# Two attention blocks in one program on one core: new set-up, a split value product, new orders at the layer change and at the end

## The reference, cut to what matters

```python
def _L0_cond_ref(x, emb, src_mask, ...):                  # H = 16 heads of 32
    xn = layer_norm(x, norm_w, norm_b)
    q = xn @ q_w + q_b ; k = xn @ k_w + k_b
    att = softmax(einsum('bnhl,bmhl->bnmh', q, k) + (1.0 - mask) * -1000000.0, axis=2)
    v = (xn @ v_w + v_b) * mask
    y = einsum('bnmh,bmhl->bnhl', att, v)
    scale, shift = split(silu(emb) @ emb_w + emb_b)
    h = layer_norm(y, sb_norm_w, sb_norm_b) * (1.0 + scale) + shift
    return x + silu(h) @ out_w + out_b

def _L1_cond_ref(x, emb, src_mask, ...):                  # H = 8 heads of 64
    q = softmax(xn @ Wq + bq, over a head's 64 features)
    k = softmax(xn @ Wk + bk + (1 - mask) * -1e6, over the tokens)
    att = einsum('bnhd,bnhl->bhdl', k, v)                 # 64 x 64 per head
    y = einsum('bnhd,bhdl->bnhl', q, att)                 # then the same tail
```

## Time and profile before

| | |
|---|---|
| time before | 1080.86 us, median of 3 runs (1080.82 to 1081.48) |
| the profiled execution | 1084.61 us, of which the span of the trace is 1082.8 us |
| TensorE busy (products) | 1030.0 us, 95% of the span, 8554 instructions |
| DVE, ACT, POOL busy | 770.1, 609.6 and 588.7 us |
| mean granted TensorE clock | 0.991 of full speed |

### The profile page before, as it was taken

The page is one execution under the profiler, slowest core; times in us unless marked ns, Lnnn a source line. Parts: engine busy times, 40 slices in busy tenths (PEclk is TensorE's granted clock), DMA queues, the critical chain, the costliest instruction groups (busy, mean ns, idle before and its releaser), DMA issues. The chain is left out here.

```text
span 1082.8 us, 26060 instructions
## 1 busy us (share of the span) xinstructions
PE 1030.0 (95%) x8554; PEld 897.0 (83%) x8554; DVE 770.1 (71%) x1349; ACT 609.6 (56%) x2018; POOL 588.7 (54%) x870
## 2 busy tenths in 40 slices
PE   2999999999999999999997899999999999999996
PEld 2678889888888888988886778888888888888885
DVE  3567666766667666676678687777887787778775
ACT  2375678766776668766694544444444444444443
POOL 3453465445654465544653576556655565666623
PEclk9999999999999999999999899999999999999999
DMA  7833102211012110111113312222111121112111
GB/s 210 283 138 120 62 26 63 63 41 61 24 63 63 41 55 30 63 54 50 43 45 112 103 44 65 64 65 63 54 39 62 53 63 53 53 63 63 44 40 39
DMA packets 46401, 74.24 MB, mean 69 GB/s; under 512 B 8304, under 2 KB 14576, under 8 KB 46352
## 3 DMA queue, kind: packets, MB, share of 16 engines
q1 hardware_dynamic: 46352, 73.63, 21.4%
HBM read 56.80 MB, written 16.81 MB: 68 GB/s over the span
## 5 line engine op out<-in xcount | busy, mean ns | idle before, releaser
L468 POOL TENSOR_SCALAR stat<-stat 128x1 f32<-128x1 f32 x128 | 34.9, 273 | 351.5 <-DVE stat L898 330.4
L1294 PE MATMUL bank<-xt_hi,w_hi 128*128 128x256 f32 x768 | 220.4, 287 | 1.5 <-DVE xt_lo L921 1.5
L1296 PE MATMUL bank<-xt_hi,w_lo 128*128 128x256 f32 x768 | 215.5, 281 | 0.0
L1295 PE MATMUL bank<-xt_lo,w_hi 128*128 128x256 f32 x768 | 215.4, 281 | 0.0
L634 ACT ACTIVATE prob<-prob,neg_max 128x128 f32<-128x128 f32 x512 | 198.5, 395 | 10.5 <-DVE neg_max L935 10.5
L1294 PE MATMUL bank<-w_hi,xt_hi 128*128 128x512 f32 x384 | 157.2, 409 | 3.6 <-DVE w_lo L859 2.0
L1296 PE MATMUL bank<-w_hi,xt_lo 128*128 128x512 f32 x384 | 151.9, 396 | 0.0
L1295 PE MATMUL bank<-w_lo,xt_hi 128*128 128x512 f32 x384 | 151.3, 394 | 0.0
L1294 PEld LDWEIGHTS bank<-xt_hi,w_hi 128*128 128x128 f32 x768 | 146.5, 191 | 5.0 <-issue 1.9
L1295 PEld LDWEIGHTS bank<-xt_lo,w_hi 128*128 128x128 f32 x768 | 146.1, 190 | 1.3
L1296 PEld LDWEIGHTS bank<-xt_hi,w_lo 128*128 128x128 f32 x768 | 145.9, 190 | 0.0
(11 more groups left out here) (113 smaller groups left out, 2341.8 us busy)
## 6 DMA issues: line engine op xcount, KB each, us to landing
x_in<-in_x_dram SPq DMA_DIRECT2D x32, 256.0 KB, 2.8
x_res<-in_x_dram SPq DMA_DIRECT2D x32, 256.0 KB, 2.9
between_layers<-x_res SPq DMA_DIRECT2D x32, 256.0 KB, 2.0
x_in<-between_layers SPq DMA_DIRECT2D x32, 256.0 KB, 3.2
x_res<-between_layers SPq DMA_DIRECT2D x30, 256.0 KB, 2.6
out_dram<-x_res SPq DMA_DIRECT2D x30, 256.0 KB, 2.0
room<-in_L_cond_W_emb_dram SPq DMA_DIRECT2D x8, 512.0 KB, 6.9
prob<-in_L_cond_emb_w_dram SPq DMA_DIRECT2D x4, 512.0 KB, 7.6
```

The source lines that it names most:

```text
L468: pool.tensor_scalar(v[:, 8:9], v[:, 7:8], EPS, None, ALU.add).then_inc(s[a_in].sem, 1)
L1294: pe.matmul(o, a_hi, b_hi, start=start, stop=False)
L1295: pe.matmul(o, a_hi, b_lo, start=False, stop=False)
L1296: return pe.matmul(o, a_lo, b_hi, start=False, stop=stop)
```

## The change

What it does, by part:

1. **Set-up.** The two norm rows are loaded by ACT's queue as one row of 2 KB each (`norm_row`) and TensorE spreads them: a product of a row of ones with the row (`ones_row`), into banks 2 and 3, from which ACT copies them to `wide` (`norm_rows_out`). SP loads both x tiles and then the weights; three other spread rows and some columns go later in its list. A first small ACT instruction (`warm`) draws the table load forward. `first_norm` does both sequences on DVE in two instructions each. The low parts of chunks 0 and 1 of the query weight move to POOL. TensorE's first queries (`first_queries`) do the four high x high products of a block first and wait for the low parts only then. Keys come ahead of the mask's transposes.
2. **Value product.** In `step0` (all 15 passes) and `step_mixed` the last of its four chunks (three matmuls of 512 columns) stands behind the last `turn_probs` of the pair, where it stood ahead of it.
3. **Change of layers.** In step 14 SP loads the x tiles of pair 17 right away, where they stood behind five other loads in step 15; the low parts of the second block's value weight move from DVE to POOL, those of its query weight are cut in two halves on ACT and DVE; in `step_mixed` DVE does both `k_soft` ahead of the second sequence's `softmax`.
4. **The end.** `drain` puts the outputs of the last two pairs later on TensorE and DVE, in other banks; the x tiles for pair 30's residual are loaded into `xn`, which is free by then, so they need not wait for a store.

The diff, cut:

```diff
@@ banks @@
-        LATE = dict(O=(5, 3))
-        LATER = dict(O=(6, 3))
-        DRAIN = SECOND | dict(V=(0, 6), Q=(2, 2), KT=(4, 5), QT=(1, 0), KV=(4, 5), Y=(2, 1), H=(0, 4), O=(5, 7))
+        LATE = dict(O=(1, 2))
+        LATER = SECOND | dict(H=(5, 7), O=(5, 6))
+        DRAIN = SECOND | dict(V=(0, 3), Q=(2, 4), KT=(6, 7), QT=(2, 4), KV=(0, 3), Y=(6, 0), H=(3, 4), O=(7, 0))
@@ SP: start @@
-                load_x(0, pair(0), 0)
-                load_norm(0)
+                load_front(0, pair(0))
                 load_weight(0, WQ)
-                load_x(0, pair(0), 1)
                 load_weight(0, WK)
-                load_wide(0, WV, VALUE_BIAS[0], par_in[0])
...
@@ SP: step0 @@
+                if i == G - 2:
+                    load_front(1, pair(G + 1))
+                    sp.wait_ge(mask_saved, 32)
+                    load_mask_pair(n)
+                    sp.wait_ge(w_split[1][WK], 1)
+                    load_weight(1, WQ)
...
                 store(0, k, 0)
@@ SP: drain @@
+                    sp.wait_ge(*done(s["xn_turned"], f + b))
+                    sp.wait_ge(*done(s["res_full"], k + (b - GROUP)))
+                    sp.dma_start(xn[:, b, :], sequence(middle, k + (b - B))).then_inc(s["res_in"][b].sem, 16)
@@ POOL @@
+            def low_part(l, j, some, last):
+                for c in some:
+                    pool.wait_ge(w_high[l][j], c + 1)
+                    low = pool.tensor_tensor(lo[l][j][:, c], raw[l][j][c // 2][:, c % 2], hi[l][j][:, c].bitcast(F32),
+                                             ALU.subtract)
+                if last:
+                    low.then_inc(w_split[l][j], 1)
@@ POOL: start @@
+                for b in range(GROUP):
+                    rsqrt(b, 0, "aggr", "rstd_a", "rstd_b", "neg_mean", pair(0) + b, "xn_turned")
+                low_part(0, WQ, (0, 1), True)
@@ POOL: step0 @@
                 v_mask(f, slot, 1)
+                if i == G - 2:
+                    low_part(1, WV, (0, 1), False)
...
                 add_shift(k, 1)
+                if i == G - 2:
+                    low_part(1, WV, (2, 3), True)
@@ ACT @@
+            for i, v in enumerate((layers[0]["nw"], layers[0]["nb"])):
+                act.dma_start(norm_row[:, i, :], v.rearrange("(o n) -> o n", o=1)).then_inc(row_in, 16)
+            act.wait_ge(once, 2)
+            act.activation(mask_now[:], minus_half[:], ACT.Identity).then_inc(warm, 1)
...
+                norm_rows_out()
+                high_part(0, WQ, (0, 1, 2))
                 xt_high(f, 0, 0)
+                high_part(0, WQ, (3,))
                 xt_high(f, 0, 1)
@@ DVE: first_norm(b) @@
+                dve.wait_ge(row_out, 1)
+                dve.scalar_tensor_tensor(out=row, in0=x_in[:, b, :], scalar=v[:, 10:11], in1=w, op0=ALU.add, op1=ALU.mult
+                dve.wait_ge(row_out, 2)
+                dve.scalar_tensor_tensor(out=row, in0=row, scalar=v[:, 9:10], in1=bias, op0=ALU.mult, op1=ALU.add
@@ DVE: step0, i == G - 2 @@
                     low_part(1, WK, (2, 3))
-                    low_part(1, WV)
@@ DVE: step_mixed @@
                 k_soft(f, slot, 0)
+                k_soft(f, slot, 1)
+                softmax(k, 1, (0, 1))
                 stats1(n, 0)
-                softmax(k, 1, (0, 1, 2))
+                softmax(k, 1, (2,))
                 output(FIRST, late + (-1), 1)
                 softmax(k, 1, (3,))
-                k_soft(f, slot, 1)
                 stats1(n, 1)
                 sums_inverse(k, 0)
+                low_part(1, WQ, (0, 1))
                 y_norm(0, k, 1 - slot, 0)
...
+                low_part(1, WQ, (2, 3))
                 film_scale(k, 0)
-                low_part(1, WQ)
@@ PE: start @@
+                for i in range(2):
+                    claim(2 + i, times(row_out, i + 1))
+                    pe.matmul(bank[2 + i][:], ones_row[:], norm_row[:, i, :], start=True, stop=True).then_inc(row_pe, 1)
                 for b in range(GROUP):
                     turn(f, b)
-                need(0, WQ)
-                queries0(f, 0, 0)
-                queries0(f, 0, 1)
+                first_queries(f)
@@ PE: step0 (step_mixed alike) @@
-                values(0, FIRST, f, slot, 0)
+                values(0, FIRST, f, slot, 0, range(C - 1))
                 turn_probs(k, 1, (2, 3))
+                values(0, FIRST, f, slot, 0, (C - 1,))
                 turn_yn(0, k, 0)
                 weigh(k, 1 - slot, 1)
@@ PE: drain @@
                 turn_k(k, 0, 1)
-                output(1, LATE, k + (-GROUP), 0)
                 keys(1, f, 1, 0)
...
                 keys_values(f, 1, 1, DRAIN)
+                turn_yn(1, k, 0, LATER)
+                turn_q(f, 1, 0, DRAIN)
+                output(1, LATE, k + (-GROUP), 0)
+                turn_q(f, 1, 1, DRAIN)
                 query(f, 0, DRAIN)
-                turn_q(f, 1, 1, DRAIN)
+                turn_yn(1, k, 1, LATER)
                 query(f, 1, DRAIN)
+                output(1, LATE, k + (-GROUP), 1)
+                turn_yn(1, f, 0, DRAIN)
                 output(1, LATER, k, 0)
-                turn_yn(1, f, 0, DRAIN)
+                turn_yn(1, f, 1, DRAIN)
                 output(1, LATER, k, 1)
```

209 lines of the change are left out of this document (118 added, 91 removed).

## The result

The changed kernel takes 1072.66 us, median of 4 runs (1071.39 to 1074.12); the kernel before took 1081.17 beside it (1080.82 to 1083.82). The ratio is 0.9924, with a 95% interval of 0.9911 to 0.9938: 8.2 us faster, where the forecast was 14.2 us and 1066.7. The time lies inside the range of 8 in 10 (1056 to 1074), 6 us above the forecast, but outside the band of 1062 to 1071 to which the forecast gave 60%; it lies in the band of "given back".

A forecast was written before the change was run, and what follows sets the result against it. The prediction took TensorE's work, 1030.0 us of a 1082.8 us span, as the bound. Its terms, -9.8 + 2.9 - 5.0 - 2.3 = -14.2 us, taken off 1080.86 gave 1066.7 us, with an 8-in-10 range of 1056 to 1074.

The forecast's parts named there:

- given back: Rival, 18%: waits at the change of layers and the end only change place, each leaving half clock; 1073.8 us.
- the two engines that hold each other up: Set-up: DVE and POOL, both reading two tiles, delay each other; 1.3 us added, to 11.4.
- it moves, it does not go: Set-up: the wait of 2.27 us at 45.15 is only moved, because DVE's next statistics stand behind the value weight's low parts.
- the output product is held by the chain from `turn_yn`: Value product passes: the tail's chain already reaches TensorE, so the output product starts 0.2 us later after waiting about 0.9.
- the switch from transposes to matmuls: Value product passes: one more such switch costs the longer spacing after a transpose, making `turn_yn` up to 0.1 us later.
- 15 passes: Value product: each of the 15 passes of `step0` loses 0.2 us, +2.9 us in all.
- passes 34.4 us apart instead of 34.2: Sign in the profile that the value product's forecast loss per pass is right.
- it loses only its idle stretch, about 2.9 us, so `turn_yn` comes at 600.5: Change of layers: POOL's untouched list sheds only idle time, bringing `turn_yn` from 603.50 to 600.5.
- which goes: Change of layers: half clock behind the 1.98 us wait disappears; it made 12 matmuls take 4.5 instead of 2.8 us.
- The half clock behind the 1.82: End: the slow clock after the 1.82 us wait, counted at 1.6 us, goes together with that wait.
- The pass does gain: Rival, 15%: the output product's 0.26 us is no wait, so passes win 0.36 each, -5.4 us; 1058.4 us.
- slower: Rival, 2%: the new 0.9 us wait lets the clock fall in every pass, +25 us; 1092 us.

The follow-up runs named there:

- second trace of before: The kernel before, unchanged, traced once more: 1080.88 us beside 1080.81, ratio 0.9998.
- the passes from 185.52 and 222.54: One pass of the kernel before with only the set-up changed (ratio 0.9908) and one of the changed kernel (0.9924), named by their start times in us.

## Why the prediction was right in sign and 6 us too far

| part | forecast, us | alone, ratio to before | in us of 1080 | read from traces, us |
|---|---|---|---|---|
| set-up | -9.8 | 0.9908 [0.9893, 0.9923] | -9.9 | -8.9 and -8.1 at the first product (first and second trace of before), -9.5 at the first `scores` (second trace) |
| value split | +2.9 | 1.0045 [1.0031, 1.0058] | +4.9 | +3.4 to +3.8 |
| change of layers | -5.0 | 0.9996 [0.9986, 1.0006] | -0.4 | -1.4 |
| end | -2.3 | 0.9973 [0.9962, 0.9984] | -2.9 | -1.3, or -2.0 where the old end had half clock |
| sum | -14.2 | | -8.3 | |
| all together | | 0.9924 [0.9911, 0.9938] | -8.2 | |

The parts add up to the whole, so each miss can be looked for in its own term. That they add up to 0.1 us is luck: each ratio is known to 1 or 1.5 us only.

**Set-up: right, with some luck in the number.** The forecast's weight at 7 us, rows at 3.6 and first product at 13.2 were 6.96 (the first half of the weight; ACT rounds it from 7.76 on, behind its copies of the rows), 3.48 and 14.05. The term that was too small is the one for the two engines that hold each other up: it was put at 1.3 us, and DVE's two instructions came to 3.34 us instead of 1.5, so 1.8 more, while POOL's two took 3.10 instead of 2.5. The Trainium skill's page "SBUF — State Buffer" (section "SBUF: two separate sides") describes for such a pair a full exclusion of one instruction by the other. The trace agrees in the direction and not in full: the four instructions take 3.64 us together (8.46 to 12.10), where one after the other they would take 4.0 and side by side 2.5. The prediction's estimate by that rule had the first product at 14.5; it came at 14.05. That -9.9 was measured against -9.8 although the first product gained less is in part the work of another place: the wait of 2.27 us at 45.15, which the forecast let stand ("it moves, it does not go"), is one of 1.46 us. The first products ran at half of their later speed until about 20.3 (213 ns from start to start, then 114), which the kernel before paid as well (until about 26 in its first trace and 28 in its second).

**Value split: right mechanism, the size of a pass half of the forecast, and one place overlooked.** The step that the output product is held by the chain from `turn_yn`, that the wait at `weigh` is only moved to it (forecast 0.9, measured 0.73), and that `v_add` ahead of `film_scale` makes the chain longer, stands. Its size doesn't: +0.11 us a pass at equal speed, forecast +0.2. The mis-sized term is the switch from transposes to matmuls, put at 0.1 us: `turn_yn` stands 24.06 us behind the pass's first `scores` with the cut and without it (the passes from 185.52 and 222.54), so the switch cost nothing, `v_add` started 0.1 us sooner than forecast, and `z_a` 0.81 us behind `turn_yn` instead of 0.74 before and of the 0.91 forecast.

The failed step is "15 passes": pass 0 isn't like the others. There the bank of `turn_yn` is read by the second embedding sum, which stands on DVE behind `v_add`; the split puts `v_add` off by the embedding products as well, and TensorE waits 1.38 us. The forecast spoke of what stands behind the waiting `v_add`, but for the loop alone. So the term of +2.9 came near the +3.4 to +3.8 of the traces by two misses that nearly cancel: the passes cost half, and pass 0 costs 1.8 to 2.2 that weren't in it. The sign that the prediction named ("passes 34.4 us apart instead of 34.2") did not show: the changed kernel's passes are 34.00 and 34.07, because its matmuls of the queries ran at the faster of their two speeds. A reader who takes that for a refutation errs, as the expectation for the split alone did.

**Change of layers: wrong, by 4.6 us in the medians, 3.6 in the traces.** The failed step is "it loses only its idle stretch, about 2.9 us, so `turn_yn` comes at 600.5": POOL's start was worked out from the DVE stall that the early load takes away, and it was not asked where on DVE the moments stand after the change. One key softmax and two softmax chunks now stand ahead of them that stood behind. Against the second trace of before (`turn_yn` at 601.85 after 2.25 us of wait) the part alone has it at 600.35, after 5.47. That 600.35 is almost the 600.5 of the forecast is chance: this trace reached the mixed step 2 us earlier, and counted from that step's first `scores`, `turn_yn` came 1.2 us earlier than in the trace the forecast was made from, and not 3. The second failed step is the half clock "which goes": with the wait that grew comes a stretch at half clock of its own (598 to 604). The wait of 1.98 for `w_lo` did go, as forecast. With the moments moved forward the part is worth 0.9956, or 4.8 us, near the forecast's 5.0.

**End: right** by the steps given, with a smaller gain than the forecast's 2.3 in the traces (1.3 to 2.0): the new wait at the keys is 1.46 (forecast 1.6), the 1.82 is gone, and of the small ones that remain the largest is 1.29 (forecast 0.7 to 1.0). The half clock behind the 1.82 was counted at 1.6 us; the second trace of before has the same wait, 1.83 at 1057.57, and full clock behind it, so this term belongs to some executions only, and cost 0.8 where it fell.

**The rivals.** What happened is nearest to "the gains in the middle and at the end are given back" (1073.8), but only its middle came true: set-up and end kept their gains in the runs. What moved the time into its band is mainly the change of layers, for which its reason (POOL's list is untouched) points at the right engine. "The pass does gain" fell with the split alone, "slower" with the trace: between 100 and 560 us the changed kernel's clock never falls.

**From trace to median.** Taking 3.75 us off for the traced execution was right: a second trace of the same kernel is 3.5 us shorter, with a granted clock of 0.997. The terms for half clock, though, were read from the trace that had more of it.

## What to carry to other kernels

An early load is worth nothing until its first reader moves as well: after a change, look up where the reader stands on its own engine, and who is behind it. A product may be cut round another step only if the step that ends last in the pass doesn't get later; here moving the longest chain (from `turn_yn`) forward brought 1.1% over the cut kernel and 0.7% over the one without the cut, where the cut by itself cost 0.45%, and the first pass has to be read on its own. And a term of 0.1 us in a pass can't be read from two traces before every unchanged stretch in them has been seen to take the same time.

## What was not expected of the hardware

The same block of 48 matmuls of 256 columns takes 7.64 or 7.83 us with what stands around it, 4 ns a matmul, with the granted clock at its full level, no gap and no wait; both occur in one execution, and what chooses between them stays open. With the keys it is up to 0.3 us a pass, about the spread between executions (1077.6 to 1084.6 us for the kernel before), though it wasn't shown that it makes that spread. In the set-up the granted clock reads 1.00 (a window of the changed kernel, third column from the end) while four matmuls from 14.05 on take 1.19 us, and the next groups of four 1.05, that take 0.62 later, so in the first 20 us the durations tell TensorE's speed and the clock column doesn't.

```profile
14.00:15.00 1.00, 0.95 (x4) 0.98 (x5) 1.00 (x2) 1.00 (x3) 0.00 (x0) 1.00 1.12 203
```
